# A selective-scan mixer: four states driven by TensorE instead of five, and another order of the steps in a chunk

## What is computed

```
xz = ln(x) @ in_proj_w.T ; xin, z = split(xz)
u  = silu(conv1d(xin) + conv_b)                    # 3 taps, per channel
dt, Bm, Cm = split(u @ x_proj_w.T)                 # 24, 16, 16 rows
dt = softplus(dt @ dt_proj_w.T + dt_proj_b)
for t:  h = exp(dt_t * A) * h + (dt_t * u_t) * B_t    # h: 768 x 16
        y_t = sum_n h[:, n] * C_t[n]
y  = (y + u * D) * silu(z)
x  = x + y @ out_proj_w.T
```

## Time and profile before

| | |
|---|---|
| median of 3 runs | 3687.05 us (3686.06 to 3687.48) |
| the profiled execution, its own time | 3687.91 us |
| its span, first to last instruction | 3686.1 us, granted clock 0.960 |
| mixer: first scan at 71.3 us, end of last scan | 2698.8 us |
| busy: TensorE, VectorE | 3304.1 us (90%), 3313.9 us (90%) |
| busy: ScalarE, GpSimd | 2733.1 us (74%), 2573.5 us (70%) |

### The profile page before, as it was taken

One profiled execution on the slowest core, in us unless ns is written; L12 is line 12 of the kernel. 1 busy time (PEld: TensorE's weight loads), 2 busy tenths in 40 slices (PEclk: granted clock), 3 DMA queues, 4 the chain that ended last, 5 costly groups with the idle time before them and its releaser, 6 DMA issues. The chain is left out here.

```text
span 3686.1 us, 48453 instructions
## 1 busy us (share of the span) xinstructions
PE 3304.1 (90%) x16194; PEld 2290.2 (62%) x16194; DVE 3313.9 (90%) x3482; ACT 2733.1 (74%) x5266; POOL 2573.5 (70%) x2045
## 2 busy tenths in 40 slices
PE   5989889898988989898999989898789998889997
PEld 2656656566566656566565666566557776557776
DVE  3999999999999999999999999999967887976886
ACT  5887787788879778877977787787655554776553
POOL 3898988989898988989898998989921111551100
PEclk7999999999999999999999999999899999999999
DMA  4020211202020211202020211202120113650112
GB/s 137 10 95 19 95 48 57 87 18 87 19 95 19 95 62 43 87 19 89 16 104 21 84 67 37 87 19 95 47 66 35 53 53 145 233 187 36 70 36 87
DMA packets 81532, 253.99 MB, mean 69 GB/s; under 512 B 15212, under 2 KB 24044, under 8 KB 71044
## 3 DMA queue, kind: packets, MB, share of 16 engines
q1 hardware_dynamic: 80516, 249.84, 18.7%
q10 hardware_dynamic: 768, 1.05, 0.1%
HBM read 208.93 MB, written 41.95 MB: 68 GB/s over the span
## 5 line engine op out<-in xcount | busy, mean ns | idle before, releaser
L956 POOL TENSOR_TENSOR slot<-dtu,b_rep 128x512 f32<-128x512 f32 x1056 | 1333.3, 1285 | 232.1 <-PE ysum L454 231.5
L454 PE MATMUL ysum<-ident,slot 128*128 128x128 f32 x6144 | 852.6, 284 | 119.9 <-DVE slot L1065 77.7
L454 PEld LDWEIGHTS ysum<-ident,slot 128*128 128x128 f32 x6144 | 733.6, 147 | 349.7 <-issue 230.2
L754 ACT ACTIVATE state<-dt,aneg 128x512 f32<-128x512 f32 x1056 | 718.3, 688 | 218.8 <-DVE slot L1065 194.2
L966 POOL TENSOR_TENSOR slot<-slot,c_rep 128x512 f32<-128x512 f32 x672 | 854.5, 1285 | 16.5 <-DVE slot L1057 8.7
L1065 DVE TENSOR_TENSOR slot<-state,c_rep 128x512 f32<-128x512 f32 x864 | 575.6, 668 | 0.0
L1057 DVE TENSOR_TENSOR_SCAN slot<-state,slot 128x512 f32<-128x512 f32 x288 | 342.7, 1203 | 27.1 <-ACT state L754 24.2
L1057 DVE TENSOR_TENSOR_SCAN slot<-state,carry,slot 128x512 f32<-128x512 f32 x288 | 360.0, 1263 | 2.5 <-ACT state L754 1.4
L745 ACT ACTIVATE slot<-dt,aneg 128x512 f32<-128x512 f32 x480 | 333.5, 709 | 6.6 <-PE ysum L454 6.6
L572 PE MATMUL state<-diag_b,dtu_t 128*128 128x128 f32 x2304 | 312.7, 280 | 15.8 <-issue 11.4
L1614 ACT ACTIVATE hid<-ph_l,bias_l 128x512 f32<-128x512 f32 x240 | 165.1, 691 | 204.2 <-PE ph_l L1425 202.8
(11 more groups left out here) (269 smaller groups left out, 6177.1 us busy)
## 6 DMA issues: line engine op xcount, KB each, us to landing
c_rep<-rows_of_b_and_c SPq DMA_DIRECT2D x64, 1024.0 KB, 4.7
xres_l<-between_layers SPq DMA_DIRECT2D x18, 1536.0 KB, 9.8
b_rep<-rows_of_b_and_c SPq DMA_DIRECT2D x32, 768.0 KB, 4.1
xn_l<-between_layers SPq DMA_DIRECT2D x13, 1536.0 KB, 7.5
b_rep<-rows_of_b_and_c SPq DMA_DIRECT2D x16, 1024.0 KB, 4.6
between_layers<-y SPq DMA_DIRECT2D x10, 1536.0 KB, 6.4
xn<-in_x SPq DMA_DIRECT2D x16, 768.0 KB, 4.4
xres<-in_x SPq DMA_DIRECT2D x16, 768.0 KB, 4.5
```

The lines of the kernel that those rows point to most:

```text
L454: last = mm(ysum[:, cols], slot[:, (NS * k + n) % SLOTS, cols], ident[:], start=first and j == 0, stop=final, is_transpose=True, skip_grou ...
L754: af(state[:, (NS * k + n) % BANKS], dt[:, k], ACT.Exp, scale=aneg[:, k, n:n + 1]).then_inc(exp_done, 1)
L956: tt(slot[:, q % SLOTS], dtu[:, k % 2], b_rep[:, b_row(n)], ALU.mult).then_inc(dbu_done, 1)
```

## The change

It changes tables of constants alone. State 13 moves from TensorE (transpose) to GpSimd, state 14 is now the one that ScalarE scales and TensorE transposes (before: with a diagonal), so TensorE drives 7 and 15 with a diagonal, 11 and 14 by a transpose. GpSimd's products with C take state 8 instead of state 7; VectorE multiplies for 7 instead of 8. Nearly all steps in the tables move, `SUM_AT` and `DT_U_AT` among them.

```diff
--- before.py
+++ after.py
@@ -26,31 +26,31 @@
 BX, BY, BZ = 0, 1, 2
 XROWS, XBC = 64, 32
 GROUP = 4
-POOL_N, POOL_LAG = (0, 1, 2, 4, 7, 9, 10), 6
-PE_N, TURN_N, SCALE_AHEAD, SCALED = (7, 11, 13, 14, 15), (11, 13), 6, 2
-SUM_AT = (6, 7, 7, 3, 8, 10, 10, 10, 12, 15, 15, 11, 14, 15, 15, 15)
-
-COPY_Y, TURN_Y_AT, GATED_Y_AT = 5, (27, 35, 51, 74, 81, 1), (32, 40, 55, 76, 84, 1)
+POOL_N, POOL_LAG = (0, 1, 2, 4, 8, 9, 10), 6
+PE_N, TURN_N, SCALE_AHEAD, SCALED = (7, 11, 14, 15), (11, 14), 6, 2
+SUM_AT = (6, 5, 5, 10, 8, 10, 10, 11, 13, 13, 15, 12, 14, 14, 15, 15)
+
+COPY_Y, TURN_Y_AT, GATED_Y_AT = 5, (29, 34, 52, 72, 81, 1), (33, 39, 60, 75, 84, 1)
 Y_IN = (BX, BZ, BY, BX, BX, BZ)
 OUT_AT, OUT_PER = (0, 1, 9), (3, 1, 1)
-OUT_IN, RES_AT = (BX, BY, BX), (9, 16, 19)
+OUT_IN, RES_AT = (BX, BY, BX), (12, 16, 20)
 LAST_OUT_IN, EARLY_OUT_AT, LATE_OUT_AT = (BX, BY, BZ), (87, 82, 84), (88, 89, 90)
 X_SUM_AT = 86
-MEAN_AT, CENTER_AT, SQUARE_AT, VAR_AT, RSTD_AT, SCALE_AT = 15, 22, 26, 23, 30, 28
-GATE_AT, GATE_IN = (20, 22, 35, 49, 64, 70), (BX, BZ, BY, BX, BY, BZ)
-IN_AT, IN_IN = (30, 32, 33, 35, 45, 47), (BY, BZ, BX, BX, BY, BZ)
-CONV_IN_AT, CONV_AT = (34, 37, 39, 48, 49, 53), (35, 36, 37, 49, 51, 52)
-SILU_AT = (31, 41, 56, 80)
+MEAN_AT, CENTER_AT, SQUARE_AT, VAR_AT, RSTD_AT, SCALE_AT = 15, 21, 25, 23, 29, 29
+GATE_AT, GATE_IN = (19, 20, 35, 46, 64, 70), (BX, BZ, BY, BX, BY, BZ)
+IN_AT, IN_IN = (30, 31, 33, 37, 44, 48), (BY, BZ, BX, BX, BY, BZ)
+CONV_IN_AT, CONV_AT = (36, 37, 40, 46, 48, 54), (34, 35, 38, 44, 49, 51)
+SILU_AT = (31, 41, 55, 79)
 SILU_CONV, SILU_GATE = ((), (0, 1, 2), (3, 4, 5), ()), ((0, 1), (2,), (3,), (4, 5))
-XP_AT, XP_COPY_AT = 51, 59
-DT_AT, DT_IN = (56, 57, 63, 70, 2, 18), (BX, BY, BZ, BX, BZ, BZ)
-DT_READ_AT = (61, 63, 73, 77, 8, 23)
-DT_ADD_AT = (66, 75, 81, 95, 10, 40)
+XP_AT, XP_COPY_AT = 54, 61
+DT_AT, DT_IN = (56, 60, 68, 70, 2, 18), (BX, BY, BZ, BX, BZ, BZ)
+DT_READ_AT = (63, 64, 73, 77, 9, 24)
+DT_ADD_AT = (72, 73, 75, 94, 34, 41)
 EARLY = 4
-DT_U_AT = 4
-TURN_U_AT, COPY_U_AT = (90, 9, 30, 39, 60, 75), (95, 18, 34, 47, 64, 85)
-TURN_B_AT, COPY_B_AT = 84, 92
-DIAG_AT = (94, 94, 0, 15, 5)
+DT_U_AT = 2
+TURN_U_AT, COPY_U_AT = (80, 8, 30, 42, 66, 75), (95, 16, 34, 50, 69, 80)
+TURN_B_AT, COPY_B_AT = 79, 82
+DIAG_AT = (94, 9, 8, 0)
 HALO_AT = 20
```

## The result

The changed kernel takes **3701.9 us** (median of 7 runs, 3698.1 to 3703.9) against 3687.5 us for the kernel before (7 runs, 3686.1 to 3690.4): ratio 1.004, 95% interval 1.003 to 1.0049. The forecast of 3665 us had the wrong sign, though the range held the time. The profiled execution's span is 3700.1 us against 3686.1, and the difference lies in the mixer: from the first scan to the end of the last 14.9 us more. Chunk 0 takes 8.4 us more (160.3 to 168.7 us). The seven chunks with h = 1 ahead of the last, the odd ones from 1 to 13, take 8.3 us more together (164.45 to 165.62 us in the mean). The even chunks from 2 to 14 hardly moved (165.59 to 165.39 us in the mean), and with the last chunk they take 1.8 us less.

A forecast was written before the change was run, and what follows sets the result against it. VectorE was taken as the bound, its idle time (about 99 us) all there is to win. Terms of -2.1 us (h = 0) and -0.65 (h = 1) a chunk, times 8, gave -22 us: 3665 us, 8 in 10 range 3616 to 3718.

The forecast's parts named there:

- Late diagonal of 14: Block 0, scans 14 and 15: state 14 no longer needs its late diagonal; gain 1.98 us with h = 0, none with h = 1.
- Sum of 3: Sum moves behind drive 7: gain 0.45 us per chunk in block 0; block 1 0.76 (h = 0), 0.4 (h = 1).
- Gate projections and centring in block 1: Block 1: centring ahead of scan 7 brings a new wait at scans 11 and 14, 1.2 us with h = 0.
- GpSimd in block 4: Block 4: two more operations make GpSimd late; loss 1.0 us with h = 0, 0.2 with h = 1.
- Copy of the turned B: Block 5, step 82: copy stands ahead of ScalarE's exp for scan 3; loss 0.3 us, bounds 0 and 1.
- the rival that GpSimd becomes the bound: GpSimd's waits return at scans 8 and 9, a chunk takes 166.7 us; 3725 us in all, chance 0.17.
- Smaller waits in block 4: Block 4: smaller waits of the same sort as scan 11's go; gain 0.5 us with h = 0.
- ScalarE costs nothing: One diagonal less a block, 1.26 us a chunk; ScalarE waits often enough that its work costs nothing.
- Block 4, scan 11: Sums 1 and 2 no longer stand ahead of drive 11: net gain 0.9 us with h = 0, 0.3 with h = 1.
- Blocks 2 and 3 with h = 1: TensorE's saved work there was taken as mostly outside the path in blocks 2 to 5; no gain or loss counted.
- Times 8: Sums per chunk, -2.1 us (h = 0) and -0.65 (h = 1), each times 8 chunks: -16.8 - 5.2 = -22 us.
- The rival of TensorE's clock: Less TensorE work puts 14 us more of a chunk at 1.2 GHz; gain eaten, about 3703 us, chance 0.10.

The follow-up runs named there:

- the last kernel: The changed kernel with three extra unread matmuls behind the turned u of block 4 and three ahead of drive 7 of block 3: 3671.4 us, 0.9959.
- The split alone: The kernel before with state 13 on GpSimd, 14 transposed, GpSimd's product of 8 instead of 7, in the old order of steps: 3690.1 us, 1.0008.
- the same run: The changed kernel with two extra unread matmuls behind the turned u of block 4: 3693.0 us, 1.0017.
- the new order with the old split: The changed kernel's steps with five states on TensorE, 13 transposed, 14 with a diagonal, GpSimd's product of 7: 3749.4 us, 1.0169.

## Why the prediction was wrong

What bounds the kernel was right: VectorE, whose busy time hardly moved, with its idle time as nearly all there was to win or lose. From the forecast of -22 us to the measured +14.9 us of the mixer are 37 us. Chunk 0 is 10.5 of them (-2.1 forecast, +8.4 measured), the seven other even chunks 13 us (-2.1 forecast, -0.2 measured in each), the odd ones from 1 to 13 another 13 us (-0.65 forecast, +1.2 measured in each). By the prediction's steps (means over the chunks of a kind, chunk 0 apart):

- *Late diagonal of 14*, -1.98 us: scans 14 and 15 went from 1.60 and 0.38 to 0. Right.
- *Sum of 3*, -0.45 us: scan 7 of block 0 lost 0.4 us of wait in every chunk but the first, block 1 0.75 and 0.57 us. Right in size, and the run with this part alone shows the same 0.4 us. What it sets off in block 4 in that run, and at scans 14 and 15 of block 0 with h = 1, was not seen.
- *Gate projections and centring in block 1*, +1.2 us: no wait came. *GpSimd in block 4*, +1.0 and +0.2 us: none came either; VectorE's waits for GpSimd fell to 1.9 us in the whole mixer. *Copy of the turned B*, +0.3 us: nothing. All three were too dear, and with them the rival that GpSimd becomes the bound falls. *Smaller waits in block 4*, -0.5 us: right, scan 9 (0.14) and the gated product (0.38) no longer wait. GpSimd's waits for sums went from 14.3 to 5.2 us a chunk with h = 0, a little under the 6 to 8 forecast.
- *ScalarE costs nothing*: **wrong** as a whole, 1.9 us a chunk more with h = 0 in blocks 3 and 4. The step looked at how often ScalarE waits, not at what stands in one piece ahead of an exp; that is 0.7 us of it. Another 0.6 us, at scan 11 of block 3, is gone in the last kernel with the pauses filled, but 0.9 us more came at scan 1 of block 4, so that the waits for ScalarE stay in sum (33.7 us in the last kernel, its start apart, 32.3 in the changed one). With the old steps of blocks 3 and 4 they fell to 0.4 us a chunk; which step it is wasn't isolated.
- *Block 4, scan 11*, -0.9 us with h = 0 and -0.3 with h = 1: **the step that failed**. With h = 1 it came true (0.32 to 0), with h = 0 the wait rose from 1.73 to 3.32 us. The step took the sums away at 0.9 us, at the fast clock, and added "It fits unless TensorE is inside a 2.7 us projection". In chunks 6 and 12 TensorE was inside one of 4.6 us. The change also left a pause of 3 us ahead of drive 7 with dt projection 2 (2.07 us) and sums 0 to 2 (2.82 instead of 1.53 us) behind it; the account of what stands behind the pause, and at which clock, was not made. The term was forecast at -0.9 us and measured at +1.6 us a chunk.
- *Blocks 2 and 3 with h = 1*: put at nothing, without a row, by "Most of that is outside the path in blocks 2 to 5". Scan 7 of block 2 and scan 11 of block 3 wait 1.25 and 1.21 us there, behind pauses that the change made or lengthened. This is the same fault as in block 4, and more than the whole miss of 1.9 us in each odd chunk. The "waits for the transposed drive of 11" in block 3 were one of the prediction's own signs of being wrong, and so was a chunk's granted clock below 0.94: chunk 0 has 0.87.
- *Times 8*: chunk 0 was taken to be like the others. It alone lost 8.4 us; scan 11 of its block 4 waits 5.0 us.

The rival of TensorE's clock, at a chance of 0.10, gave 3703 us and is what came; but half of its reason was not right. It had the clock fall because the split takes work out of each block. The split alone does lower it (0.962 to 0.952), yet the time stays the same. The size was luck: granted clocks of 0.94 and 0.96 are 6.5 to 10 us more of a chunk at 1.2 GHz, not 14, and the even chunks hardly got longer. What decides is on which group the slow time falls. In the kernel before, a slow gate projection 4 in odd chunks delayed nobody; with sum 3 moved, projection 5 is the slow one, and drive 11 waits for that. The section "HAM oscillation — how this bites in real kernels" of "TensorE: Matmul & The Clock Gate" in the Trainium skill says that bursts behind a long wait start at the slow clock, and advises to order the loops so that the engine stays busy. The traces agree in the main: with 3.30, 2.16 and 1.30 us of pause ahead of drive 7 in chunk 6, drive 7 to gate projection 5 took 12.4, 9.1 and 7.5 us. They also show that the length of the pause doesn't settle it: behind 2.16 us three other chunks of the same run took 12.4 us too, behind 1.30 us two chunks with three matmuls took 9 us, and in the last kernel the turned y of block 2 took 1.12 us in chunk 1 and 1.87 us in chunk 3, both behind 2.46 us. What settles it beside the pause stays open. That useless matmuls are worth issuing is what the runs here add.

The last kernel is 14.8 us faster than the one before, where the forecast was 22. But a fill helps the kernel before as well (3680.8 us): with both filled, each at the places that were tried, the change is worth 9.4 us. The waits for ScalarE are one part of what is lacking. Which pause brings 1.2 GHz in the odd chunks of block 2 (0.9 us at scan 7 there, still) wasn't tried.

## What to carry to other kernels

When an edit takes a wait away or work out of a stretch, look at what the engine's pauses become and at the longest matmul group behind them, at both of its durations (here 2.84 and 4.54 us), before adding up gains. Where a loss can't be placed, fill the pause right ahead of the slow group with matmuls that nobody reads: if the group is back at its fast duration and the kernel gets faster, it was the clock, and the fill may stay. Look at all chunks and not at one: the same pause gave both durations here. Count each chunk that differs from the rest, the first above all, by itself.

## What the hardware showed that was not expected

- A move of one sum (0.45 us of work) costs 25 us of 3686, and two useless matmuls (1.88 us in each chunk) bring 25 us back.
- The same six matmuls took 2.84, 4.54 and 5.49 us, behind pauses in the slow cases, but 2.84 and 4.25 us behind one and the same pause of 1.84 us.
- The split alone lowers the mean granted clock from 0.962 to 0.952 and the time stays; the new order with the old split has 0.955 and is 59 us slower. On which group the slow stretch falls says more than the mean.
- A fill must be of work that doesn't prolong the pause: 24 transposes ahead of a copy that waits for them left 2.99 us of pause, two to three ordinary matmuls behind them shortened it.
- GpSimd at 157 of 165 us a chunk didn't slow itself (1275 ns a product against 1285), and VectorE's product rose from 668 to 672 ns, 3.6 us in all.
